# Both halves of an odd unit's transposes ahead of the sum over n, in a selective-scan block

## Chip, cores, metric

The program runs on one core of a Trainium2 chip. The metric is the device time of one execution in microseconds (us); a kernel is judged by the median of its runs.

## What is computed

For each of 16 batches (512 time steps, 256 features) the reference takes a layer norm with a shift and scale from a condition, then two Mamba blocks, one over time forward and one over time reversed, sums and norms them, and adds a gated feed-forward net of four layers. Most of the time goes into the scan of the two Mamba blocks, with E = 512 channels and N = 64 states each:

```python
def step(h, inp):
    xt, dtt, Bt, Ct = inp
    dA = jnp.exp(dtt[:, :, None] * A)
    h = dA * h + (dtt * xt)[:, :, None] * Bt[:, None, :]
    y = jnp.einsum('ben,bn->be', h, Ct)
    return (h, y)
```

So for every channel e, state n and time t: a decay exp(dt A), a drive (dt x) B, the recurrence over t, a product with C, and a sum over n.

## The kernel before

**Tiles.** A tile holds 32 channels x 4 states on the 128 partitions, and 512 time steps along the free axis. A *unit* is four such tiles (128 channels, 4 states); a *half* is two of them (1024 columns). 16 units make a pass (128 channels, all 64 states), 8 passes make a batch: 4 groups of channels for each direction, 128 units and 256 halves in all. The program has a short body ahead of the first batch, bodies for the first and the last batch, one after the last, and a hardware loop over the 14 batches between.

**One unit, over the engines.** Each engine runs its own list of instructions in the order in which they are written, and waits on counters (semaphores) of the others.

- ACT (ScalarE) writes the decays of a unit into `state[unit % 4]` (line 1078), two units ahead.
- The drive comes in one of two ways. For an even unit DVE (VectorE) multiplies rows of dt x by rows of B that TensorE has spread over the partitions into the PSUM tile `b_ps` (`spread`, line 872; the multiply is line 1256). For an odd unit ACT and POOL (GpSimd) form the product in another layout, `v_sb` (lines 1091 and 1364), and TensorE (PE) transposes it into place: eight 128x128 transposes for each half (`drive` of the tensor engine, line 882). Both ways write the PSUM tile `driven`, which has two slots: slot h for half h of any unit.
- DVE scans each half in place in `state` (line 1267); the scan of half h frees slot h of `driven`.
- POOL multiplies the scanned half by rows of C (line 1297).
- PE sums over n into the PSUM tile `y_ps` with a 0/1 matrix (`accumulate`, line 904: eight instructions for a unit) and counts `summed`, which frees the unit's slot of `state` for the decays of the unit four later.

**The order around the change.** DVE's list goes: the two scans of an even unit, the two of the odd unit behind it, then both multiplies for the next even unit. So an odd unit's first transposed half can be written once the even unit's first scan is done, its second half once the second is, and DVE needs them for its third and fourth scan of the pair. PE's list is written by `body` (line 908). At an even unit it holds: the first half of the next odd unit's transposes, the sum of the unit before, the second half, the `spread` for the next even unit, and then side work (`side`: the projections of another batch and the feed-forward net of the previous one, spread over the units by a table). At an odd unit: the sum of the even unit, and side work. Where a pass begins (`unit % NG == 0`, `ends_pass` in the code) the sum stands ahead of both halves, since DVE must read the finished `y_ps` (line 1193) before it goes on.

`accumulate` waits until POOL has read the unit (`was_read`); `drive` waits for the scan that frees its slot:

```python
pe.wait_ge(scanned, of_body(at, HALVES, last_user(q, DRIVE_RING, HALVES) + 1) + DRIVE_RING)
...
pe.wait_ge(was_read, read_done(at, unit))
```

ACT's first part of `v_sb` for a later odd unit waits for the second half of an earlier one (`v_free`), since `v_sb` has two slots.

Of the kernel before, what the change touches and what calls it, by code (L numbers as in the profile page):

```python
# [213 lines left out]
def adaln_kernel(nc, x, win, wxp, wdt, wout, f1, h1, h2, w3, cols, rows, c_t, wmod, consts, spread_rows, out):  # L214
    ctx = ExitStack()
    with ctx:
# [163 lines left out]
        def of_body(at, per_body, index):  # L380

            return at.b * per_body + index

        def last_user(k, ring, count):

            if k >= ring:
                return k - ring
            return max(r for r in range(count) if r % ring == k) - count
# [25 lines left out]
        def v_count(at, unit):  # L414

            return of_body(at, len(PE_UNITS), len([u for u in PE_UNITS if u <= unit]))
# [268 lines left out]
        def _(pe):  # L685
# [165 lines left out]
            def side(at, unit):  # L851
                for steps, signal, emit in ((PE_Q, pe_q, network), (PE_P, pe_p, project)):
                    for s, part, name, n in steps:
                        if s != unit or not at.has(part):
                            continue
                        first = min(x[0] for x in steps if x[1:3] == (part, name))
                        mm = emit(at, part, name, s - first)
                        if n:
                            mm.then_inc(signal.sem, 1)

            def spread(at, unit):
                d, g = unit % UNITS // (UNITS // 2), unit % NG
                if unit == 0:
                    pe.wait_ge(dve_side.sem, dve_side.before(at))
                elif unit == UNITS:
                    pe.wait_ge(dve_side.sem, dve_side.done(at, "next", "BC"))
                elif unit == UNITS // 2:
                    pe.wait_ge(dve_side.sem, dve_side.done(at, "p1", "BC"))
                pe.wait_ge(dve_driven, dve_drives(at, unit, 0) - 1)
                quarter = N // NN // NN  # L870
                k = slice(EG * (g // quarter), EG * (g // quarter + 1))
                pe.matmul(b_ps[:], onehot[k, g % quarter, :], b_parts[d][k, :], start=True, stop=True).then_inc(b_spread, 1)  # L872

            def drive(at, unit, h):
                q = 2 * unit + h
                if h == 0:
                    pe.wait_ge(v_made, v_count(at, unit))
                    pe.wait_ge(v_pooled, v_count(at, unit))
                pe.wait_ge(scanned, of_body(at, HALVES, last_user(q, DRIVE_RING, HALVES) + 1) + DRIVE_RING)
                for j in (2 * h, 2 * h + 1):  # L880
                    for tt in range(TT):
                        mm = pe.transpose(driven[:, q % DRIVE_RING, j % 2, tt * P:(tt + 1) * P],  # L882
                                          v_sb[:, unit // 2 % V_RING, tt, j].rearrange("p e n -> p (e n)"), ident)
                mm.then_inc(pe_driven, 1)

            def accumulate(at, unit):
                k = unit % UNITS
                nth, g = k // NG, k % NG
                if g == 0:
                    if nth:  # L890
                        pe.wait_ge(dve_side.sem, dve_side.done(at, "o0", f"Y{(nth - 1) // EC}{(nth - 1) % EC}"))
                    elif at.kind != "first":
                        pe.wait_ge(dve_side.sem, dve_side.done(at, "early", "Y13"))
                    d, c = nth // EC, nth % EC
                    if c == 0:
                        pe.wait_ge(skip_in.sem, skip_in.done(at, "o0", "skip1") if d else skip_in.before(at))
                        if d:
                            pe.wait_ge(pool_side.sem, pool_side.done(at, "p1", "ub"))
                        else:
                            pe.wait_ge(pool_side.sem, pool_side.before(at))  # L900
                    pe.matmul(y_ps[:], skip_w[:, c, :], xc_sb[d][:, c, :], start=True, stop=False)
                pe.wait_ge(was_read, read_done(at, unit))
                for j in range(JC):
                    mm = pe.matmul(y_ps[EG * j:EG * (j + 1), :], over_nn, state[:, k % STATE_RING, j, :],  # L904
                                   start=False, stop=(g == NG - 1))
                mm.then_inc(summed, 1)

            def body(at):
                scans = at.kind in SCAN_PARTS
                if at.kind == "first":  # L910
                    spread(at, 0)
                for unit in range(UNITS):
                    before_scans = unit == 0 and at.kind in ("mid", "last", "tail")
                    to_drive, ends_pass = scans and unit + 1 in PE_UNITS, unit % NG == 0
                    if to_drive and not ends_pass:
                        drive(at, unit + 1, 0)
                    if before_scans or scans and unit:
                        accumulate(at, unit - 1)
                    if to_drive and ends_pass:
                        drive(at, unit + 1, 0)  # L920
                    if to_drive:
                        drive(at, unit + 1, 1)
                        if unit + 2 < UNITS:
                            spread(at, unit + 2)
                        elif at.has("next"):
                            spread(at, unit + 2)
                    side(at, unit)

            bodies(pe, body)


# [499 lines left out]
```

## Time and profile before

| | |
|---|---|
| median of three runs | 12842.57 us |
| lowest, highest | 12838.57, 12843.2 us |
| span of the profiled execution (first to last instruction) | 12820.6 us |
| the profiled execution's own time | not given apart from its span |
| time outside the span, against the median | 22 us |
| DVE busy | 11937.2 us, 93% |
| POOL busy | 11387.8 us, 89% |
| ACT busy | 10827.8 us, 84% |
| PE busy, matmuls | 10193.9 us, 80% |
| mean granted clock of PE | 0.898 |

A page tells the busy time of each engine, and for groups of instructions how long the engine stood idle ahead of them and what ended that. Idle time matters where the engine that waits is the one that sets the pace. The timeline lists instructions by their start, each with the idle time before it. The granted clock is 1 where PE runs at its upper level and 0.5 where it runs at its lower.

### The profile page before, as it was taken

To read this page: it belongs to the slowest core of one execution; us is meant where nothing else is said; L and a number is where in the kernel's file an instruction comes from. 1 tells how busy PE (TensorE), PEld (TensorE's weight loads), DVE (VectorE), ACT (ScalarE), POOL (GpSimd) and SP (SyncE) were. 2 spreads that over 40 slices of the span, in tenths; PEclk is the share of its full clock that TensorE was granted. 3 is DMA by queue.
4 is the path that set the end of the run, shared out by engine and by line. 5 is a ranking of instruction groups with operands and counts; after the bars stand their busy time and mean duration, and the time that the engine had idled before them with its cause. 6 is when DMAs were issued, how large, how long until landed. Compare 5 with 4: busy or idle time off the path is not lost.

```text
span 12820.6 us, 179717 instructions
## 1 busy us (share of the span) xinstructions
PE 10193.9 (80%) x51484; PEld 5804.4 (45%) x51484; DVE 11937.2 (93%) x7080; ACT 10827.8 (84%) x23460; POOL 11387.8 (89%) x5924
## 2 busy tenths in 40 slices
PE   5667878888787887878878788887878878788777
PEld 2334544445444454544445444454444545444445
DVE  5999999999999999999999999999999999999992
ACT  5788888888888898888888888888888988888882
POOL 4889999999999999999998999999999999999992
PEclk7788989899898998989989898998989989899898
DMA  2223333333333343433333333333433334333332
GB/s 87 81 85 110 124 109 125 125 105 113 115 127 114 114 126 98 130 115 119 123 108 118 112 126 122 107 118 108 128 114 118 122 105 130 111 122 119 112 109 98
DMA packets 610266, 1459.04 MB, mean 114 GB/s; under 512 B 68928, under 2 KB 110032, under 8 KB 604672
## 3 DMA queue, kind: packets, MB, share of 16 engines
q1 hardware_dynamic: 609152, 1446.18, 35.3%
q8 instruction: 456, 7.47, 0.2%
q14 instruction: 658, 5.39, 0.1%
HBM read 1355.09 MB, written 90.83 MB: 113 GB/s over the span
## 4 chain that ended last, share of the span: by engine, by line
PE 28%; issue 25%; ACT 18%; DVE 18%; POOL 9%; DMA 1%; DVEq 0%; SPq 0%; POOLq 0%; ACTq 0%
DVE state L1267 11%; PE driven L882 10%; POOL state L1297 7%; ACT state L1078 6%; ACT v_sb L1091 6%; PE y_ps L904 5%; PE q_ps L837 4%; DVE driven L1256 4%; PE q_ps L824 2%; PE p_ps L745 2%; PE b_ps L872 1%; PE p_ps L753 1%; PE p_ps L769 1%; ACT L1078 1%; PE p_ps L760 1%
## 5 line engine op out<-in xcount | busy, mean ns | idle before, releaser
L1297 POOL TENSOR_TENSOR state<-state,c_rep 128x1024 f32<-128x1024 f32 x4096 | 9717.2, 2401 | 979.1 <-DVE state L1267 975.9
L1267 DVE TENSOR_TENSOR_SCAN state<-state,driven 128x1024 f32<-128x1024 f32 x4096 | 9104.4, 2270 | 405.2 <-PE driven L882 352.2
L1078 ACT ACTIVATE state<-ud_rep,cols_sb 128x512 f32<-128x512 f32 x8192 | 5211.6, 710 | 2.6 <-DMA ud_rep<-ud_rows 0.4
L1091 ACT ACTIVATE v_sb<-u_t,b_t 128x128 f32<-128x128 f32 x12288 | 4064.7, 505 | 1303.2 <-PE driven L882 1299.8
L882 PE MATMUL driven<-consts_sb,v_sb 128*128 128x128 f32 x16384 | 2641.8, 314 | 1670.0 <-DVE state L1267 1624.8
L882 PEld LDWEIGHTS driven<-consts_sb,v_sb 128*128 128x128 f32 x16384 | 2130.3, 161 | 3299.2 <-DVE state L1267 2199.8
L904 PE MATMUL y_ps<-state,consts_sb 128*32 128x512 f32 x16384 | 2452.4, 674 | 313.1 <-POOL state L1297 310.9
L1256 DVE TENSOR_TENSOR driven<-ud_rep,b_ps 128x1024 f32<-128x1024 f32 x2048 | 2390.4, 1213 | 18.2 <-DMA ud_rep<-ud_rows 18.2
L837 PE MATMUL q_ps<-hid,wq_sb 128*128 128x256 f32 x7936 | 2044.5, 403 | 140.6 <-ACT hid L1056 77.3
L837 PEld LDWEIGHTS q_ps<-hid,wq_sb 128*128 128x128 f32 x7936 | 1477.3, 196 | 838.1 <-issue 649.9
L1364 POOL TENSOR_TENSOR v_sb<-u_t,b_t 128x512 f32<-128x512 f32 x1024 | 1090.0, 1064 | 38.4 <-issue 25.4
L904 PEld LDWEIGHTS y_ps<-state,consts_sb 128*32 128x32 f32 x16384 | 338.4, 113 | 1142.1 <-POOL state L1297 643.2
L824 PE MATMUL q_ps<-xn_q,wq_sb 128*128 128x256 f32 x1984 | 518.7, 407 | 32.7 <-ACT hid L1046 19.0
L753 PE MATMUL p_ps<-u_pad,dt_sb 128*128 128x512 f32 x1024 | 508.8, 621 | 26.2 <-ACT u_pad L980 25.7
L745 PE MATMUL p_ps<-x_t,wp_sb 128*128 128x512 f32 x1024 | 500.1, 612 | 30.2 <-ACT xc L984 17.4
L872 PE MATMUL b_ps<-b_parts,onehot 32*128 32x512 f32 x1024 | 519.3, 507 | 0.0
L824 PEld LDWEIGHTS q_ps<-xn_q,wq_sb 128*128 128x128 f32 x1984 | 373.5, 198 | 221.7 <-issue 99.1
L847 PE MATMUL q_ps<-wq_sb,hid 128*128 128x256 f32 x992 | 274.6, 425 | 69.7 <-ACT hid L1061 66.1
L753 PEld LDWEIGHTS p_ps<-u_pad,dt_sb 128*128 128x128 f32 x1024 | 186.4, 195 | 239.6 <-issue 184.1
L745 PEld LDWEIGHTS p_ps<-x_t,wp_sb 128*128 128x128 f32 x1024 | 187.7, 192 | 230.5 <-issue 150.7
L790 PE MATMUL p_ps<-sz 16*128 16x512 f32 x256 | 175.1, 769 | 145.8 <-ACT u_pad L1010 145.3
L872 PEld LDWEIGHTS b_ps<-b_parts,onehot 32*128 32x128 f32 x1024 | 191.6, 187 | 186.7 <-issue 186.7
(141 smaller groups left out, 5538.1 us busy)
## 6 DMA issues: line engine op xcount, KB each, us to landing
c_rep<-bc_rows SPq DMA_DIRECT2D x2048, 256.0 KB, 3.0
ud_rep<-ud_rows SPq DMA_DIRECT2D x512, 512.0 KB, 4.1
wq_sb<-in_h SPq DMA_DIRECT2D x512, 512.0 KB, 3.7
wq_sb<-in_f SPq DMA_DIRECT2D x128, 512.0 KB, 4.2
wp_sb<-in_win SPq DMA_DIRECT2D x64, 512.0 KB, 4.5
dt_sb<-conv_taps SPq DMA_DIRECT2D x32, 1024.0 KB, 5.2
ud_rows<-u_pad SPq DMA_DIRECT2D x128, 256.0 KB, 3.4
ud_rows<-dt_sb SPq DMA_DIRECT2D x128, 256.0 KB, 3.5
```

What stands on the lines that cost most here:

```text
L745: mm = pe.matmul(p_ps[:], wp_sb[:, m, k, :], x_t[:, k, :], start=(k == 0), stop=(k == DC - 1))
L824: mm = pe.matmul(bank[:, which * TH:(which + 1) * TH], w[:, m % 2, which, k, :], n_t[:, k, i * TH:(i + 1) * TH], start=(k == 0), stop=(k = ...
L837: mm = pe.matmul(bank[:, 0:TH], w[:, k, :], src[:, k, :], start=(k == 0), stop=(k == HC - 1))
L872: pe.matmul(b_ps[:], onehot[k, g % quarter, :], b_parts[d][k, :], start=True, stop=True).then_inc(b_spread, 1)
L882: mm = pe.transpose(driven[:, q % DRIVE_RING, j % 2, tt * P:(tt + 1) * P], v_sb[:, unit // 2 % V_RING, tt, j].rearrange("p e n -> p (e n)" ...
L904: mm = pe.matmul(y_ps[EG * j:EG * (j + 1), :], over_nn, state[:, k % STATE_RING, j, :], start=False, stop=(g == NG - 1))
L1078: ins = act.activation(state[:, unit % STATE_RING, j, :], ud_rep[:, nth % 2, j, 1, :], ACT.Exp, scale=a_neg[:, d, c, j, g:g + 1])
L1091: ins = act.activation(v_sb[:, unit // 2 % V_RING, tt, :, :, n].rearrange("p j e -> p (j e)"), u_t[:, nth % 2, tt, :], ACT.Identity, scale ...
L1256: dve.tensor_tensor(driven[:, h], u_rows(unit)[:, 2 * h:2 * h + 2], b_ps[:].unsqueeze(1).to_broadcast([P, 2, T]), ALU.mult).then_inc(dve_d ...
L1267: dve.tensor_tensor_scan(flat, flat, driven[:, q % DRIVE_RING].rearrange("p j t -> p (j t)"), 0.0, ALU.mult, ALU.add).then_inc(scanned, 1)
L1297: pool.tensor_tensor(part, part, c_rep[:, unit % ROW_RING, :].unsqueeze(1).to_broadcast([P, 2, T]), ALU.mult).then_inc(was_read, 1)
L1364: pool.tensor_tensor(v_sb[:, unit // 2 % V_RING, TT - 1].rearrange("p j e n -> p (j e) n"), u_t[:, nth % 2, TT - 1, :].unsqueeze(2).to_bro ...
```

## The change

In the tensor engine's list, at an even unit that does not begin a pass, the second half of the transposes moves from behind the sum to directly behind the first half. At units that begin a pass the order stays as it was. Nothing else changes: the same instructions with the same waits.

```diff
--- before.py
+++ after.py
@@ -914,12 +914,13 @@
                     to_drive, ends_pass = scans and unit + 1 in PE_UNITS, unit % NG == 0
                     if to_drive and not ends_pass:
                         drive(at, unit + 1, 0)
+                        drive(at, unit + 1, 1)
                     if before_scans or scans and unit:
                         accumulate(at, unit - 1)
                     if to_drive and ends_pass:
                         drive(at, unit + 1, 0)
+                        drive(at, unit + 1, 1)
                     if to_drive:
-                        drive(at, unit + 1, 1)
                         if unit + 2 < UNITS:
                             spread(at, unit + 2)
                         elif at.has("next"):
```

PE in the loop over the middle batches, units 10 and 11 (`driven` is written by the transposes, `y_ps` by the sum, `b_ps` by `spread`; the last matmuls into `p_ps` are side work, and REGISTER_ALU rows work out values to wait for). Before:

```order
L879 REGISTER_ALU
L882 MATMUL driven<-consts_sb,v_sb 128x128 x8
L902 REGISTER_ALU
L904 MATMUL y_ps<-state,consts_sb 32x512 x4
L882 MATMUL driven<-consts_sb,v_sb 128x128 x8
L869 REGISTER_ALU
L872 MATMUL b_ps<-b_parts,onehot 128x512
L782 ISA
L784 MATMUL p_ps<-consts_sb,u_nat 128x128 x4
L902 REGISTER_ALU
L904 MATMUL y_ps<-state,consts_sb 32x512 x4
```

And with the change:

```order
L879 REGISTER_ALU
L882 MATMUL driven<-consts_sb,v_sb 128x128 x8
L879 REGISTER_ALU
L882 MATMUL driven<-consts_sb,v_sb 128x128 x8
L904 MATMUL y_ps<-state,consts_sb 32x512 x4
L869 REGISTER_ALU
L872 MATMUL b_ps<-b_parts,onehot 128x512
L782 ISA
L784 MATMUL p_ps<-consts_sb,u_nat 128x128 x4
L902 REGISTER_ALU
L904 MATMUL y_ps<-state,consts_sb 32x512 x4
```

The second group of eight transposes has passed the four-fold sum of unit 9; the spread, the side work and the sum of unit 10 keep their places behind it.

PE in the same loop, units 82 and 83, where side work of both kinds follows (`q_ps` belongs to the feed-forward net, `p_ps` to the projections). Before:

```order
L882 MATMUL driven<-consts_sb,v_sb 128x128 x8
L902 REGISTER_ALU
L904 MATMUL y_ps<-state,consts_sb 32x512 x4
L882 MATMUL driven<-consts_sb,v_sb 128x128 x8
L869 REGISTER_ALU
L872 MATMUL b_ps<-b_parts,onehot 128x512
L714 REGISTER_ALU
L824 MATMUL q_ps<-xn_q,wq_sb 128x256 x4
L714 REGISTER_ALU
L741 REGISTER_ALU
L745 MATMUL p_ps<-x_t,wp_sb 128x512 x2
```

And with the change:

```order
L882 MATMUL driven<-consts_sb,v_sb 128x128 x8
L879 REGISTER_ALU
L882 MATMUL driven<-consts_sb,v_sb 128x128 x8
L904 MATMUL y_ps<-state,consts_sb 32x512 x4
L869 REGISTER_ALU
L872 MATMUL b_ps<-b_parts,onehot 128x512
L714 REGISTER_ALU
L824 MATMUL q_ps<-xn_q,wq_sb 128x256 x4
L714 REGISTER_ALU
L741 REGISTER_ALU
L745 MATMUL p_ps<-x_t,wp_sb 128x512 x2
```

Again only the sum and the second half have changed places; the side work now follows the sum and the spread.

## Rows read from the trace of the kernel before

**Rows 1.** Page of the profile, its head and busy time of each engine.

```profile
span 12820.6 us, 179717 instructions
PE 10193.9 (80%) x51484; PEld 5804.4 (45%) x51484; DVE 11937.2 (93%) x7080; ACT 10827.8 (84%) x23460; POOL 11387.8 (89%) x5924
```

**Rows 2.** Waits, whole run: who <- whom, us in total, times, longest.

```profile
PE driven L882 <- DVE state L1267: 1624.8, 745, 10.1
ACT v_sb L1091 <- PE driven L882: 1299.8, 521, 7.4
...
DVE state L1267 <- PE driven L882: 352.2, 464, 3.0
```

**Rows 3.** Groups by line: busy us, mean ns | idle before <- releasers.

```profile
L1297 POOL TENSOR_TENSOR state<-state,c_rep 128x1024 f32<-128x1024 f32 x4096 | 9717.2, 2401 | 979.1 <-DVE state L1267 975.9
...
L1078 ACT ACTIVATE state<-ud_rep,cols_sb 128x512 f32<-128x512 f32 x8192 | 5211.6, 710 | 2.6 <-DMA ud_rep<-ud_rows 0.4
```

**Rows 4.** Waits of DVE in the seventh batch, 4827.7 to 5605 us.

```profile
DVE state L1267 <- PE driven L882: 22.7, 27, 3.0
```

**Rows 5.** Timeline, units 10 and 11: start, us, instruction [idle before <- releaser].

```profile
4887.28 2.39 POOL L1297 TENSOR_TENSOR state<-state,c_rep 128x1024 f32<-128x1024 f32 x1
...
4889.44 6.64 DVE L1267 TENSOR_TENSOR_SCAN state<-state,driven 128x1024 f32<-128x1024 f32 x3
...
4891.78 1.97 PE L882 MATMUL driven<-consts_sb,v_sb 128*128 128x128 f32 x8 [5.64 <-DVE state L1267]
...
4893.68 1.94 PE L904 MATMUL y_ps<-state,consts_sb 128*32 128x512 f32 x8
...
4895.55 1.97 PE L882 MATMUL driven<-consts_sb,v_sb 128*128 128x128 f32 x8
...
4897.45 0.54 PE L872 MATMUL b_ps<-b_parts,onehot 32*128 32x512 f32 x1
4897.56 2.29 DVE L1267 TENSOR_TENSOR_SCAN state<-state,driven 128x1024 f32<-128x1024 f32 x1 [1.48 <-PE driven L882]
4897.56 2.58 ACT L1091 ACTIVATE v_sb<-u_t,b_t 128x128 f32<-128x128 f32 x8 [4.71 <-PE driven L882]
...
4900.46 1.93 ACT L1078 ACTIVATE state<-ud_rep,cols_sb 128x512 f32<-128x512 f32 x3
```

**Rows 6.** Timeline, same batch: first and last wait ahead of a fourth scan.

```profile
4847.15 2.29 DVE L1267 TENSOR_TENSOR_SCAN state<-state,driven 128x1024 f32<-128x1024 f32 x1 [0.91 <-PE driven L882]
...
5564.70 2.29 DVE L1267 TENSOR_TENSOR_SCAN state<-state,driven 128x1024 f32<-128x1024 f32 x1 [0.27 <-PE driven L882]
```

**Rows 7.** Waits of DVE in units 0 to 15, 4827.7 to 4928.7 us.

```profile
DVE state L1267 <- PE driven L882: 5.8, 5, 1.5
```

**Rows 8.** Windows, units 0-15, 80-95: us, PE PEld DVE ACT POOL, PEclk.

```profile
4827.70:4928.70 101.00, 70.98 (x334) 37.00 (x326) 94.70 (x60) 72.67 (x169) 94.20 (x54) 0.75 0.38 122
...
5318.00:5424.00 106.00, 96.94 (x485) 54.15 (x484) 101.23 (x58) 98.17 (x214) 99.89 (x48) 0.98 0.40 122
```

**Rows 9.** Timeline of units 82 to 84, a packed pair.

```profile
5330.35 8.81 DVE L1267 TENSOR_TENSOR_SCAN state<-state,driven 128x1024 f32<-128x1024 f32 x4
...
5332.69 1.09 PE L882 MATMUL driven<-consts_sb,v_sb 128*128 128x128 f32 x8 [0.69 <-DVE state L1267]
...
5333.71 1.06 PE L904 MATMUL y_ps<-state,consts_sb 128*32 128x512 f32 x8
...
5341.33 8.81 DVE L1267 TENSOR_TENSOR_SCAN state<-state,driven 128x1024 f32<-128x1024 f32 x4
...
5344.50 1.03 PE L882 MATMUL driven<-consts_sb,v_sb 128*128 128x128 f32 x8
```

**Rows 10.** Timeline of PE, first and last packed first half of the batch.

```profile
5001.43 1.04 PE L882 MATMUL driven<-consts_sb,v_sb 128*128 128x128 f32 x8
...
5539.03 1.04 PE L882 MATMUL driven<-consts_sb,v_sb 128*128 128x128 f32 x8
```

**Rows 11.** Line 1267 by itself: idle before it until, us, times.

```profile
  ACT state L1078: 10.4, 24
```

## The prediction

> **What bounds the kernel now.** The first view is the page's list of engines: VectorE (DVE) is busy 11937.2 of 12820.6 us, 93%, more than any other engine [rows 1]. What is worth having is therefore what DVE waits for. The second view, the waits over the whole run, gives it: DVE's scans stood still for 352.2 us, in 464 places, until a bank of `driven` had been filled by TensorE (PE) [rows 2]. That is the most that this change can win. The third view, the groups by line, tells who is not in the way: POOL waited 975.9 us for DVE's scans, so it has room for a faster DVE, and ACT's decays waited for next to nothing (2.6 us) [rows 3].
>
> The fourth view is the timeline. The batches of the middle body are alike, so I take one, the seventh (4827.7 to 5605 us), and multiply by 16: its DVE waits for PE come to 22.7 us in 27 places [rows 4], times 16 is 363, against 352.2 for the run. I call two units, an even one and the odd one behind it, a pair: DVE runs four scans (even 0, even 1, odd 0, odd 1) and two multiplies for the next even unit. A wait ahead of the third scan is a wait for the first half of the transposes, one ahead of the fourth for the second half.
>
> The pair of units 10 and 11 shows the second kind [rows 5]. The first scan starts at 4889.44; three scans in 6.64 us with a step of 2.18 put the ends at 4891.72, 4893.90 and 4896.08. PE transposes the first half from 4891.78 in 1.97 us, does the sum of unit 9 (line 904) from 4893.68 in 1.94, and only at 4895.55 begins the second half, 1.65 us after its bank was free. It ends at 4897.5, and DVE has sat idle for 1.48 us. In the batch there are 15 such waits ahead of a fourth scan, from 0.91 at unit 3 to 0.27 at unit 121 [rows 6]; they sum to 11.2 us. In units 0 to 15 nothing else holds DVE up for PE: 5.8 us in 5 places [rows 7]. The other 12 waits, 11.5 us, stand ahead of a third scan.
>
> The clock tells the two kinds of pair apart. In units 0 to 15 the granted clock was 0.75, in units 80 to 95 0.98 [rows 8]. Eight transposes take 1.97 us at the lower level (1.2 GHz) and 1.09 at the upper (2.4 GHz), the sum 1.94 and 1.06 [rows 5, 9]. At the upper level first half and sum end 2.1 us after the first scan, within the 2.18 of the second, and the second half is not late.
>
> **What the change removes.** Outside a pass's first unit, the second half follows the first at once, and the sum stands behind both. For units 10 and 11 the second half would run from 4893.96 to 4895.93, ahead of 4896.08: the wait is gone. The other 14 have the same form, and 11.2 x 16 = **179 us** go. Where a unit begins a pass, both halves already stand together behind the sum, and nothing moves.
>
> **What it adds.** No instruction is added or dropped; the sum and the matmul of line 872 (`spread`) behind it come later. There are three prices.
>
> First, PE no longer fills its wait for the second scan with the sum. In rows 5 PE sits idle for 5.64 us up to 4891.78, although POOL's last read of unit 9 ended at 4889.67 (4887.28 + 2.39): the sum was ready 2.1 us earlier and did not pass the transposes ahead of it. So what stands behind a waiting transpose waits too. The Trainium skill says the same and speaks against this change: "TensorE: Matmul & The Clock Gate", under "Step-by-step: what each phase is for", has it that only weight loads are pulled ahead while matmuls keep program order; were the sum free to slip forward, this price would be nothing and the change would give the full 179 us.
>
> At the upper level the delay is one sum, 1.06 us, for all that PE does until the next pair. In most pairs PE then has idle time that takes it up (1624.8 us over the run waiting for scans [rows 2]). In a packed pair it has none. Units 82 and 83: before their first half PE waits 0.69 us, and after it there is no idle time until the next first half, at 5344.50 instead of the 5343.61 at which its bank was free (5341.33 + 2.28) [rows 9]. That half ends at 5345.53, 0.26 ahead of the second scan (5341.33 + 2.28 + 2.18 = 5345.79). Delayed by 1.06 it is 0.80 late, and DVE pays that. In the batch five first halves follow on so packed a stretch: those for units 29, 33, 85, 101 and 117, the first at 5001.43 and the last at 5539.03 [rows 10]. I price them at 1.06, 1.06, 0.80, 1.06 (0.80, and the remaining 0.26 one pair later) and 0.80, with 0.26 more for a delay that is carried on: 5.0 us, times 16 is **81 us**. The bounds are nothing, if the short waits of PE for ACT inside these stretches shrink by as much, and twice as much, if five more pairs that have only such waits to give pay as well. I take the middle, since rows 9 hold no idle time at all.
>
> Second, the sum delays `spread`, and DVE's multiply needs its result. At the lower level the new order has the second half end at 4895.93, the sum at 4897.8 and `spread` (0.54) at 4898.4; the fourth scan, without its wait, ends at 4898.26. That is a new wait of 0.15 us. Only pairs that stay at the lower level throughout pay it, which are those with a wait near the 1.48 of rows 5, four of the 15: 0.6 us, times 16 is **10 us**; the bounds are 0 and 15 x 0.15 x 16 = 36.
>
> Third, the sum releases the state slot that ACT's decays fill next. In rows 5 the sum of unit 9 ends at 4895.62 and the decays that need its slot begin at 4900.46, 4.8 us later. The delay is 2.2 us at the lower level, so I cost it at nothing: ACT's own order covers it. If ACT came sooner, DVE would still have its lead. ACT also gains: it waited 4.71 us for the second half there, and 1299.8 over the run [rows 2, 5]; that shortens a wait, and DVE does not wait for that work. POOL's and SP's queues are passed by nothing that moves.
>
> **Sum.** -179 + 81 + 10 = -88 us. The profiled execution's span is 12820.6; the median of the runs, 12842.57, lies 22 us above it, and I take that remainder as unchanged: 12842.6 - 88 = **12755 us**.
>
> **Rivals.** *(A) The delay is absorbed everywhere.* ACT gets its buffers earlier, PE waits less for ACT in the packed stretches, and only the gain stays: 12842.6 - 179 = 12664. For it speak ACT's 1299.8 us of waiting; against it the rows without any idle time. Chance 0.16.
>
> *(B) Ten packed pairs instead of five.* Then 161 us go back, and -179 + 161 + 10 = -8: 12835, no change. For it speaks that PE waited for DVE in only 745 places ahead of a half [rows 2], of 2048 halves in the run (16 batches of 64 pairs), so PE often has no idle time to give; against it, that many of the others had waits for POOL or ACT in between. Chance 0.14.
>
> *(C) ACT becomes the wait: slower.* Side work of an even unit now leaves PE 1.06 us later at the upper level, ACT stands in order behind it, and the decays queued behind that eviction come late for the scan. DVE has waited for decays already, 10.4 us in 24 places [rows 11], so in some units their lead is small. It decides from 6 places a batch on (88 / 1.06 / 16 = 5.2); at 8 it costs 8 x 1.06 x 16 = 136 us, and the time is 12842.6 - 88 + 136 = 12891. Against it: the decays themselves waited for nobody [rows 3], and 10.4 us is little beside 352.2. Chance 0.08.
>
> *(D) The clock falls in a packed pair.* PE now pauses about 1.0 us between the halves at the upper level. In units 80 to 95 it was busy 96.94 of 106 us [rows 8], some 10 us a pair; transposes and sums take 0.9 us more at the lower level per group of eight, and with all of its work so stretched such a pair would last some 7 us longer. One a batch costs 112 us: 12842.6 - 88 + 112 = 12867. Before the change these stretches hold the upper level, and the pause is shorter than the 5.64 us that preceded lower-level transposes [rows 5]. The skill's same page, under "A second HAM failure mode: psum-queue depth-cycling", reports frequent small idles between groups of matmuls as a cause of a swinging clock; by that rule this rival would be the likely one. Chance 0.05.
>
> **How the numbers follow.** The forecast has the rest, 0.57. What a measurement here can tell from no change is about 0.2%, 26 us. The forecast and A lie beyond that on the fast side, 0.73; B and D, at -8 and +24, are within it, 0.19; C is slower, 0.08. The range takes in A, B and the bounds of the second price, and leaves C, D and little else outside: 12655 to 12838.
>
> **What would show it.** In the profile after, DVE's waits ahead of a fourth scan are gone, and its waits for `driven` fall from 352.2 to about 254 us (352.2 - 179 + 81). They all stand ahead of a third scan, more of them in units 82 to 118. DVE gets a new wait of some 10 us ahead of line 1256's counterpart, for `b_ps`. PE waits longer in all before its second halves and less before its first. ACT's wait at `v_sb` shrinks. I am wrong if DVE's waits for ACT's decays grow by over 88 us, if the granted clock of units 80 to 95 falls below 0.9, or if waits ahead of a third scan grow past 350.

## The result and the profile after

The changed kernel took **12886.86 us** (median of five runs, 12879.91 to 12894.58) against 12838.57 of the kernel before beside it: a ratio of 1.0038, 95% interval 1.0026 to 1.0051. It is slower by 48 us, where 88 less were predicted; the time lies outside the range given.

The head of the page after, and from its fifth part the group of DVE's scans (busy us, mean ns, then idle us ahead and its releaser):

```profile
span 12885.1 us, 179717 instructions
PE 10259.9 (80%) x51484; PEld 5938.8 (46%) x51484; DVE 11996.8 (93%) x7080; ACT 10879.2 (84%) x23460; POOL 11351.8 (88%) x5924
...
L1268 DVE TENSOR_TENSOR_SCAN state<-state,driven 128x1024 f32<-128x1024 f32 x4096 | 9083.3, 2269 | 330.4 <-PE driven L882 259.9
```

Its waits over the whole run, to be laid beside [rows 2]:

```profile
PE driven L882 <- DVE state L1268: 1837.8, 1281, 10.1
...
ACT v_sb L1092 <- PE driven L882: 1015.0, 394, 7.2
...
DVE state L1268 <- PE driven L882: 259.9, 268, 3.1
```

What was forecast for the transposes happened. DVE's waits for `driven` fell from 352.2 us in 464 places [rows 2] to 259.9 in 268; 254 was forecast. In units 0 to 15 of the seventh batch, where [rows 7] had 5.8 us, none is left. ACT waits 285 us less at `v_sb`. Yet the span is 64.5 us longer (12885.1 against 12820.6). That is more than the 48 us between the medians, since the kernel before was profiled in an execution quicker than its median. DVE sets the pace, so the place to look is DVE's other instructions. Of the kernel before, by line:

```profile
L1193 DVE TENSOR_TENSOR xc<-y_ps,sz 128x512 f32<-128x512 f32 x128 | 86.4, 675 | 16.6 <-PE y_ps L904 16.5
...
L1217 DVE TENSOR_TENSOR xa<-xa,mod_p 128x1024 f32<-128x1024 f32 x16 | 45.9, 2869 | 5.7 <-ACT xa L963 5.7
...
L1223 DVE TENSOR_TENSOR o_sb<-o_sb,mod_q 128x1024 f32<-128x1024 f32 x16 | 29.6, 1852 | 5.6 <-ACT o_sb L963 5.6
...
L1238 DVE SCALAR_TENSOR_TENSOR u_pad<-sz,u_pad 128x2048 f32<-128x2048 f32 x32 | 78.2, 2445 | 65.8 <-ACT sz L1016 65.8
L1240 DVE TENSOR_TENSOR dt_sb<-dt_sb,u_pad 128x2048 f32<-128x2048 f32 x32 | 108.1, 3378 | 1.1
```

And after:

```profile
L1194 DVE TENSOR_TENSOR xc<-y_ps,sz 128x512 f32<-128x512 f32 x128 | 86.5, 676 | 55.8 <-PE y_ps L904 55.8
...
L1218 DVE TENSOR_TENSOR xa<-xa,mod_p 128x1024 f32<-128x1024 f32 x16 | 38.3, 2396 | 22.4 <-ACT xa L964 22.4
...
L1224 DVE TENSOR_TENSOR o_sb<-o_sb,mod_q 128x1024 f32<-128x1024 f32 x16 | 90.7, 5671 | 5.6 <-ACT o_sb L964 5.6
...
L1239 DVE SCALAR_TENSOR_TENSOR u_pad<-sz,u_pad 128x2048 f32<-128x2048 f32 x32 | 113.5, 3547 | 67.6 <-ACT sz L1017 67.6
L1241 DVE TENSOR_TENSOR dt_sb<-dt_sb,u_pad 128x2048 f32<-128x2048 f32 x32 | 85.7, 2678 | 1.1
L1257 DVE TENSOR_TENSOR driven<-ud_rep,b_ps 128x1024 f32<-128x1024 f32 x2048 | 2394.1, 1215 | 36.4 <-DMA ud_rep<-ud_rows 18.4 <-PE b_ps L872 15.6
```

The account of DVE's 64.5 us, from these lines:

| | us |
|---|---|
| scans' waits for `driven` | -92.3 |
| multiply waits for `b_ps` (none shown before) | +15.6 |
| line 1224 (`mix`) is itself longer, 29.6 to 90.7 busy | +61.1 |
| line 1194 waits for `y_ps` | +39.3 |
| line 1218 waits for ACT | +16.7 |
| lines 1239 and 1241 together | +12.9 |
| all else, by difference | +11.2 |

The first two were forecast, at -98 and +10. The next two, `mix` and `y_ps`, were not, and are more than the whole gain.

**`mix`.** It multiplies the block's output by a row once a batch, behind unit 15; both inputs lie in SBUF. POOL's *reads* are its products of a scanned half with rows of C (line 1297 before, 1298 after). DVE and POOL there in the seventh batch, before (start, us, instruction):

```profile
4922.95 4.69 POOL L1297 TENSOR_TENSOR state<-state,c_rep 128x1024 f32<-128x1024 f32 x2
4926.10 2.63 DVE L1223 TENSOR_TENSOR o_sb<-o_sb,mod_q 128x1024 f32<-128x1024 f32 x1
4927.61 2.02 POOL L1364 TENSOR_TENSOR v_sb<-u_t,b_t 128x512 f32<-128x512 f32 x1
```

And after:

```profile
4915.28 2.40 POOL L1336 TENSOR_TENSOR x_q<-x_q,xn_q 128x1024 f32<-128x1024 f32 x1
4917.60 4.71 POOL L1298 TENSOR_TENSOR state<-state,c_rep 128x1024 f32<-128x1024 f32 x2
4917.71 6.68 DVE L1224 TENSOR_TENSOR o_sb<-o_sb,mod_q 128x1024 f32<-128x1024 f32 x1
4922.24 1.06 POOL L1365 TENSOR_TENSOR v_sb<-u_t,b_t 128x512 f32<-128x512 f32 x1
```

Before, `mix` started late in POOL's reads and ended 1.1 us after them. After, it started 0.1 us behind the first of two reads and ended 1.1 us after the third POOL instruction (4923.30). No idle time is booked ahead of it: the time stands in the instruction's own duration.

**`y_ps`.** PE around units 30 to 32 of the same batch, before:

```profile
5014.34 1.09 PE L882 MATMUL driven<-consts_sb,v_sb 128*128 128x128 f32 x8 [1.47 <-DVE state L1267]
5015.36 1.06 PE L904 MATMUL y_ps<-state,consts_sb 128*32 128x512 f32 x8
5016.52 1.09 PE L882 MATMUL driven<-consts_sb,v_sb 128*128 128x128 f32 x8
```

After, with DVE's line 1194, which needs the pass's finished `y_ps`:

```profile
5010.62 1.09 PE L882 MATMUL driven<-consts_sb,v_sb 128*128 128x128 f32 x8 [1.47 <-DVE state L1268]
5012.80 1.52 PE L882 MATMUL driven<-consts_sb,v_sb 128*128 128x128 f32 x8 [1.08 <-DVE state L1268]
5014.25 1.94 PE L904 MATMUL y_ps<-state,consts_sb 128*32 128x512 f32 x8
...
5025.09 1.07 PE L904 MATMUL y_ps<-state,consts_sb 128*32 128x512 f32 x8
...
5026.23 0.69 DVE L1194 TENSOR_TENSOR xc<-y_ps,sz 128x512 f32<-128x512 f32 x1 [2.49 <-PE y_ps L904]
```

Before, PE worked without idle time: half 1.09, sum 1.06, half 1.09, all at the upper level. After, it pauses 1.08 us between the halves; the second half takes 1.52, between the 1.09 and 1.97 of the two levels, and the sum 1.94, which is the lower level's [rows 5]. PE has no idle time from there to the sum of unit 31, so that one is late too, by more than 1.06 us, and DVE waits 2.49 us for it at unit 32. Of the 55.8 us of these waits 34.9 are at unit 32, where there was none before.

The stretch that the prediction watched for this shows nothing of it (units 0 to 15 and 80 to 95, columns as in [rows 8]): 0.98 in units 80 to 95, as before. For the whole run the clock went from 0.898 to 0.891.

```profile
4825.00:4926.00 101.00, 68.95 (x326) 37.33 (x326) 100.02 (x61) 73.32 (x169) 93.12 (x53) 0.77 0.36 120
5320.00:5426.00 106.00, 95.59 (x484) 53.97 (x482) 100.73 (x57) 97.55 (x213) 98.09 (x48) 0.98 0.37 119
```

### The profile page after: what moved, and what is told of

Its sections match the earlier page's. It is cut to its first block, busy times and chain, and to the rows that moved or that the text cites. A ratio compares the mean times of both kernels' runs of the same rounds, so it can differ in the third digit from the quotient of the medians.

```text
span 12885.1 us, 179717 instructions
## 1 busy us (share of the span) xinstructions
PE 10259.9 (80%) x51484; PEld 5938.8 (46%) x51484; DVE 11996.8 (93%) x7080; ACT 10879.2 (84%) x23460; POOL 11351.8 (88%) x5924
## 4 chain that ended last, share of the span: by engine, by line
PE 27%; issue 27%; DVE 20%; ACT 20%; POOL 5%; DMA 1%; DVEq 1%; SPq 0%; POOLq 0%; ACTq 0%
DVE state L1268 13%; ACT state L1079 7%; PE driven L882 6%; ACT v_sb L1092 6%; PE q_ps L837 5%; PE y_ps L904 5%; POOL state L1298 4%; DVE driven L1257 4%; PE q_ps L824 2%; PE p_ps L745 2%; PE b_ps L872 2%; PE p_ps L753 1%; ACT L1079 1%; PE p_ps L760 1%; PE p_ps L769 1%
## 5 line engine op out<-in xcount | busy, mean ns | idle before, releaser
L1268 DVE TENSOR_TENSOR_SCAN state<-state,driven 128x1024 f32<-128x1024 f32 x4096 | 9083.3, 2269 | 330.4 <-PE driven L882 259.9
L882 PE MATMUL driven<-consts_sb,v_sb 128*128 128x128 f32 x16384 | 2733.8, 325 | 1860.5 <-DVE state L1268 1837.8
L882 PEld LDWEIGHTS driven<-consts_sb,v_sb 128*128 128x128 f32 x16384 | 2260.8, 168 | 2656.2 <-DVE state L1268 2180.8
L904 PE MATMUL y_ps<-state,consts_sb 128*32 128x512 f32 x16384 | 2391.0, 659 | 178.9 <-POOL state L1298 178.0
L1257 DVE TENSOR_TENSOR driven<-ud_rep,b_ps 128x1024 f32<-128x1024 f32 x2048 | 2394.1, 1215 | 36.4 <-DMA ud_rep<-ud_rows 18.4
L1057 ACT ACTIVATE hid<-q_ps,cols_sb 128x256 f32<-128x256 f32 x496 | 226.3, 456 | 203.8 <-PE q_ps L837 201.7
L1047 ACT ACTIVATE hid<-q_ps,cols_sb 128x256 f32<-128x256 f32 x496 | 204.0, 463 | 102.5 <-PE q_ps L824 99.6
```

Source lines behind the costliest of these rows:

```text
L1257: dve.tensor_tensor(driven[:, h], u_rows(unit)[:, 2 * h:2 * h + 2], b_ps[:].unsqueeze(1).to_broadcast([P, 2, T]), ALU.mult).then_inc(dve_d ...
L1268: dve.tensor_tensor_scan(flat, flat, driven[:, q % DRIVE_RING].rearrange("p j t -> p (j t)"), 0.0, ALU.mult, ALU.add).then_inc(scanned, 1)
```

## The experiments

Twelve kernels, in three groups of four, each with the kernel before beside it (12825.13, 12826.84 and 12831.79 us). Most apply the new order at a list of units only:

```diff
                     if to_drive and not ends_pass:
                         drive(at, unit + 1, 0)
+                        if unit in BOTH_AT:
+                            drive(at, unit + 1, 1)
...
                     if to_drive:
-                        drive(at, unit + 1, 1)
+                        if ends_pass or unit not in BOTH_AT:
+                            drive(at, unit + 1, 1)
```

| kernel | new order at | other edit | us | ratio, 95% |
|---|---|---|---|---|
| before_nomix | none | no `mix` | 12754.35 | 0.9924 to 0.9957 |
| after_nomix | all | no `mix` | 12810.02 | 0.9978 to 0.9997 |
| low1 | 2 to 14 | | 12801.16 | 0.9965 to 0.9988 |
| low2 | 12 units from 20 to 120 | | 12916.85 | 1.0052 to 1.0086 |
| low1_no14 | 2 to 12 | | 12799.57 | 0.9972 to 0.9991 |
| low1_pre16 | 2 to 14 | `pre2` later | 12779.72 | 0.9952 to 0.9977 |
| before_pre16 | none | `pre2` later | 12781.07 | 0.9958 to 0.998 |
| low2_fill | as low2 | pause filled | 13043.74 | 1.0154 to 1.0188 |
| only30 | 30 | | 12869.9 | 1.0019 to 1.004 |
| only30_fill | 30 | pause filled | 12847.88 | 1.0002 to 1.0021 |
| after_mixbn | all | `mix` to bn_stats | 12817.99 | 0.9976 to 0.9995 |
| pre16_4u | 2, 4, 10, 12 | `pre2` later | 12782.05 | 0.9947 to 0.9976 |

### `mix` left out, in both orders

```diff
-                    emit(dve.tensor_tensor(o_sb[:], o_sb[:], over_tiles(mod_q[:, 0, :]), ALU.mult), True)
+                    emit(dve.memset(o_sb[:, 0, 0:1], 0.0), True)
```

> Order of before; the row multiplication called mix (DVE, unit 15) is left out, a memset of one column stands in its place. Theory P (a DVE instruction with both inputs in SBUF is held out while POOL runs its reads back to back): the 16 mixes took 29.6 us of DVE, so at most 29 us go, 12811 us, or less if POOL's backlog shows at the next such instruction. Theory T (only TensorE's lateness costs): the same 29 us.

> Order of the change, mix left out in the same way. P: the 90.7 us that the 16 mixes took after the change go, 12887 - 90 = 12797 us, and the change is then no slower than the kernel before without mix (about -14 us against 12811). T: mix only sat in time that was lost anyway, so the change stays about 48 us slower than the kernel before without mix, near 12860.

Neither theory had these times: in the old order 71 us went, where 29 were the most expected, and in the new order the time lies between those of P and T. Without `mix` the new order is still 55.7 us slower than the old (12810.02 - 12754.35). So the lengthening of `mix` is a real part of DVE's account, but not the sole cause. With it gone, line 1194 waits 57.0 us for `y_ps` against 12.2 without the new order, and line 1218 27.8 us for ACT against 5.7.

The 57.0 us lie elsewhere than the 55.8 of the changed kernel: 18.4 are at unit 16, where that one waits for nothing, and 15.3 at unit 32. At unit 30 of after_nomix PE pauses as before, yet here the second half keeps the upper level:

```profile
4988.09 1.09 PE L882 MATMUL driven<-consts_sb,v_sb 128*128 128x128 f32 x8 [1.47 <-DVE state L1268]
4990.27 1.09 PE L882 MATMUL driven<-consts_sb,v_sb 128*128 128x128 f32 x8 [1.08 <-DVE state L1268]
```

So it is in 14 of the 15 batches behind the first, and the wait at unit 32 is 0.93 or 0.94 us in each of the 14. The pause alone does not decide whether the clock falls.

### Early units alone, later low-clock units alone

> New order only at units 2 to 14 of a batch, old order elsewhere. Before, 5.8 us a batch of waits ahead of a fourth scan stood there. P: they go, but DVE then reaches mix ahead of POOL's reads and waits there instead; mix grows from 1.9 us to 5 or 6, and the time stays at 12840 within 20 us. T: 5.8 x 16 = 93 us go, 12747 us.

> New order only at units 20, 22, 36, 38, 44, 52, 60, 66, 70, 74, 106 and 120, old order elsewhere. About 5.4 us a batch of waits ahead of a fourth scan stood there, 87 us in all. P: they go, less some 14 us at the instructions with two SBUF inputs of unit 40: 12767 us. T: all 87 us, 12753 us. Both expect a clear gain.

Low1 gains 24 us, between the 93 of T and the nothing of P, and outside the bounds of both. In its profile, of an execution that took 12825.57 us and so gained nothing, pairs 2, 4, 10 and 12 are shorter by 0.57, 0.73, 1.03 and 0.73 us (mean of 14 batches); pair 14 is longer by 2.83, `mix` being 5.5 us there, as P had it.

Low2 was chosen where DVE had waited for second halves, so it should have gained. Those waits shrank (idle time ahead of fourth scans 177 us to 107), but those ahead of third scans grew by more (218 to 293), and it is 0.7% slower, at a mean clock of 0.879. By line, the waits that grew most besides are line 1221's for ACT's norm (47.4 us against 5.7) and the multiply's for `b_ps` (26.9 against none). PE from unit 66 of the seventh batch in low2 (line 883 the transposes, 905 the sum, 838 side work):

```profile
5273.87 1.20 PE L883 MATMUL driven<-consts_sb,v_sb 128*128 128x128 f32 x8 [4.42 <-DVE state L1271]
5276.05 1.97 PE L883 MATMUL driven<-consts_sb,v_sb 128*128 128x128 f32 x8 [0.97 <-DVE state L1271]
5277.95 1.93 PE L905 MATMUL y_ps<-state,consts_sb 128*32 128x512 f32 x8
...
5280.53 3.78 PE L838 MATMUL q_ps<-hid,wq_sb 128*128 128x256 f32 x8
```

And before:

```profile
5234.48 1.97 PE L882 MATMUL driven<-consts_sb,v_sb 128*128 128x128 f32 x8 [4.43 <-DVE state L1267]
5236.38 1.94 PE L904 MATMUL y_ps<-state,consts_sb 128*32 128x512 f32 x8
5238.25 1.40 PE L882 MATMUL driven<-consts_sb,v_sb 128*128 128x128 f32 x8
...
5240.00 1.99 PE L837 MATMUL q_ps<-hid,wq_sb 128*128 128x256 f32 x8
```

Before, PE worked without a pause from the first half on and came back to the upper level during the second half (1.40). In low2 it paused 0.97 us, and second half, sum, spread and side work all ran at the lower level; the side group took 3.78 us and not 1.99. In pair 68, behind it, ACT's norm is then late for line 1221 by 2.98 us. That gave theory K: the pause costs clock, and the lateness is paid in the next pairs. These rows do not show it by themselves, since the first half took 1.20 us in low2, over the 1.09 of the upper level: the clock was falling ahead of the pause, behind 4.42 us without work.

### Which unit brings `mix` to its bad place, and POOL's backlog

`PRE_AT` sets the units of three pieces of POOL's early work:

```diff
-O1_AT, MIX_AT, N_AT, PRE_AT = 3, 15, 24, (5, 7, 14)
+O1_AT, MIX_AT, N_AT, PRE_AT = 3, 15, 24, (5, 7, 16)
```

> The new order at units 2, 4, 6, 8, 10 and 12 alone (the run with unit 14 as well took 12801.2 against 12825.1 of the kernel before; there pairs 2 to 12 were shorter by 0.57, 0.73, 0.06, 0, 1.03 and 0.73 us, and pair 14 longer by 2.83). Theory P (at unit 14 the DVE multiplication mix, both of whose inputs are in SBUF, now starts among POOL's reads and takes 5.7 us in place of 1.9): without unit 14 mix keeps its 1.9 us, and 12801.2 - 2.83 x 16 = 12756 us, against 12825 about 0.994 to 0.995. Rival L (time won is given back at the next fixed obstacle, mix only being the first): the time stays at about 12801, the give-back appears at unit 14 or 16 all the same.

> The new order at units 2 to 14, and POOL's third piece of early work (pre2) two units later, behind mix. Theory P with POOL's backlog as the cause (POOL is busy 94 of 101 us in units 0 to 15, so its reads run back to back when mix starts): 2.4 us less backlog lets mix start in a gap, mix falls from 5.7 towards 2 us, pair 14 gets its gain of 0.84 as well: 12801.2 - (2.83 + 0.84) x 16 = 12742 us. Rival P2 (two reads of POOL in a row catch mix whatever the backlog): mix stays over 5 us and the time near 12801.

> Control: the order of before, with pre2 two units later. Theory P: mix was 1.9 us and its floor is 1.2 to 1.4, so at most 0.6 x 16 = 10 us are won: 12815 to 12830. If POOL's backlog in units 0 to 15 held DVE in some other way as well, more is won.

> A version that might beat both: pre2 two units later (12781.1 by itself) and the new order at units 2, 4, 10 and 12 alone, where the pairs were shorter by 0.8, 1.2, 1.4 and 0.4 us. If mix stays below 3 us: 12781 - 3.8 x 16 + 1.6 x 16 = 12746. Rival R (POOL sets the pace of units 0 to 15: what DVE gains there it loses at mix): about 12780, mix near 3.8 us.

The mean of `mix` by kernel: 1.85 us before, 5.48 in low1, 4.69 in low1_no14, 3.79 in low1_pre16, 3.64 in pre16_4u, 1.37 in before_pre16. Leaving unit 14 alone did not save it: 12799.57, where P expected 12756 and rival L about 12801. So it is not one unit's order: in each of the kernels where DVE gains in units 2 to 12, `mix` is long, which fits with DVE's advance over POOL as the cause. Less backlog on POOL shortens it, but not to 2 us, as theory P had it, nor does it stay over 5, as P2 had it: 3.79 and 3.64. (L names two different rivals in these runs, as each text says.)

Rival R of the last run gave both its numbers (12780 and 3.8), but not for its reason, that DVE loses at `mix` what it gains. By the profiles, pairs 2 to 12 of pre16_4u are 3.6 us a batch shorter than those of before_pre16 and pair 14 is only 1.0 longer. What cancels the rest are 3.0 us at later pairs, whose order is the same in both, such as 38 and 68 (0.73 and 0.74); the mean granted clock is 0.898 and 0.903. That POOL sets the pace of units 0 to 15 is not shown.

Moving `pre2` helps by itself, by more than the control's expectation (12815 to 12830): 12781.07 against 12826.84. `mix` is only 8 us of it ((1852 - 1367) ns x 16); by the profiles 15 us are waits for `driven` (337.5) and 19 are line 1217 (26.9 busy against 45.9). None of the gain lies in units 0 to 17, which together keep their length within 0.1 us a batch; 4.0 us a batch lie later, 1.5 of them at pair 68, while the granted clock went from 0.898 to 0.903. Why these later places improved was not tried. On top of it the new order at early units adds nothing: 12779.72 and 12782.05. All three beat both kernels, and the smallest edit does it.

### The pause filled

Four repeats of `spread`'s matmul between the halves; the real one overwrites their result:

```diff
                         if unit in BOTH_AT:
+                            filler(at, unit + 2, 4)
                             drive(at, unit + 1, 1)
...
+            def filler(at, unit, times):
+                pe.wait_ge(dve_driven, dve_drives(at, unit, 0) - 1)
+                d, g = unit // (UNITS // 2), unit % NG
+                k = slice(EG * (g // (N // NN // NN)), EG * (g // (N // NN // NN) + 1))
+                for _ in range(times):
+                    pe.matmul(b_ps[:], onehot[k, g % (N // NN // NN), :], b_parts[d][k, :], start=True, stop=True)
```

> The new order at units 20, 22, 36, 38, 44, 52, 60, 66, 70, 74, 106 and 120, with four repeats of the matmul that spreads B (its result is written over later by the real one) between the two halves there. Without the repeats this set took 12916.9 us at a mean granted clock of 0.879, and the second halves at units 60, 66, 70, 74, 106 and 120 all ran at the lower level. Theory K (it is the pause between the halves that keeps TensorE at the lower level; second half, sum and the side group behind them then take twice as long and the next pairs are late): with the pause filled the clock is back to 0.893 or more, side groups of 8 take 2.0 us and not 3.8, pair 68 loses its 2.8 us, and the time falls to 12825 to 12860, the fourth-scan waits being back. Rival L (the lateness of the sum and of what is queued behind it is the cause): the repeats make all of that later by 1 to 2 us more, so the time is 12917 or above.

This missed in its time, 13043.74, and in its clock, 0.875. At unit 66 the fill took 2.07 us, since the clock had already begun to fall in the first half, and so it made the second half late itself: DVE's waits for `driven` rose from 359.2 to 513.1. Behind that, the side group is back to 1.99 us:

```profile
5319.08 2.07 PE L892 MATMUL b_ps<-b_parts,onehot 32*128 32x512 f32 x4
5321.08 1.97 PE L883 MATMUL driven<-consts_sb,v_sb 128*128 128x128 f32 x8
5322.98 1.94 PE L912 MATMUL y_ps<-state,consts_sb 128*32 128x512 f32 x8
...
5325.45 1.99 PE L838 MATMUL q_ps<-hid,wq_sb 128*128 128x256 f32 x8
```

The time is what rival L had (12917 or above), the side group what K had, and the fill changed both at once, so it does not decide between them. The clean place is pair 30, which stands at the upper level and has no wait to win.

> The new order at unit 30 alone, the last but one pair of a pass, where no wait ahead of a fourth scan is to be won. Theory K (the pause between the halves drops TensorE to its lower level; second half and sum then take about 0.9 and 0.7 us more, on top of the 1.06 of the moved sum, and the finished y_ps that DVE needs at unit 32 is 2.6 us late): pair 32 is longer by 2.4 us as in the changed kernel, 2.4 x 14 to 16 = 34 to 38 us, so 12860 to 12865 against 12827, about 1.0028. Rival A (pair 32 of the changed kernel is late because of what happened in units before 30): the time stays within 10 us of the kernel before.

> The same, with four repeats of the matmul that spreads B between the two halves (1.25 us at the upper level in an earlier run, so that they fit in the pause of 1.08 us within 0.2). Theory K: with the pause filled the second half takes 1.09 us and the sum 1.07, only the 1.06 us of the moved sum are left, and the wait at unit 32 shrinks from 2.5 to about 1 us: 12827 + 0.9 x 15 = 12840. Rival L (the order alone makes the sum late): as long as without the repeats, 12860 to 12865, since the repeats shorten nothing.

Both times came close to theory K. The order alone is 38 us above the kernel before beside it (33 to 38 expected) and the filled one 16 (13 expected), where rival L had no gain from the fill. PE and line 1197 or 1205 around pair 30 of the seventh batch, the order alone:

```profile
5026.10 1.09 PE L883 MATMUL driven<-consts_sb,v_sb 128*128 128x128 f32 x8 [1.46 <-DVE state L1271]
5028.28 1.50 PE L883 MATMUL driven<-consts_sb,v_sb 128*128 128x128 f32 x8 [1.09 <-DVE state L1271]
5029.71 1.94 PE L905 MATMUL y_ps<-state,consts_sb 128*32 128x512 f32 x8
...
5041.70 0.69 DVE L1197 TENSOR_TENSOR xc<-y_ps,sz 128x512 f32<-128x512 f32 x1 [2.49 <-PE y_ps L905]
```

And filled:

```profile
5023.06 1.20 PE L892 MATMUL b_ps<-b_parts,onehot 32*128 32x512 f32 x4
5024.21 1.09 PE L883 MATMUL driven<-consts_sb,v_sb 128*128 128x128 f32 x8
5025.24 1.06 PE L912 MATMUL y_ps<-state,consts_sb 128*32 128x512 f32 x8
...
5036.06 0.69 DVE L1205 TENSOR_TENSOR xc<-y_ps,sz 128x512 f32<-128x512 f32 x1 [0.93 <-PE y_ps L912]
```

More work between the halves made the wait shorter, 0.93 for 2.49. The batches behind the first split the same way within each kernel: in only30 nine of 15 had a second half of 1.5 us or more and a wait of 2.36 to 2.49, the other six had 1.09 and 0.93 to 0.94. With the fill, the lower level came in two of 15; in the changed kernel, in twelve; before, in none. So of the 2.49 us, 0.93 is the moved sum and the rest the clock.

### `mix` with one input

```diff
-                    emit(dve.tensor_tensor(o_sb[:], o_sb[:], over_tiles(mod_q[:, 0, :]), ALU.mult), True)
+                    for tt in range(TT - 1):
+                        dve.bn_stats(stats[:, 1, tt, :], o_sb[:, tt, :])
+                    emit(dve.bn_stats(stats[:, 1, TT - 1, :], o_sb[:, TT - 1, :]), True)
```

> The changed kernel with mix (o_sb times a row, both from SBUF) replaced by four bn_stats over the same 1024 columns of o_sb, which have one input; the multiplication with the row is left out. Theory P (an instruction of DVE with two inputs in SBUF stands still while POOL's reads follow one another, one with a single input does not): the four take 0.4 us each, 1.6 together, in place of 5.7, and the time is 12887 - 4 x 16 = 12820 to 12825. Rival Q (any DVE instruction at this place is slowed by POOL's traffic): they take 4 us or more together and the time stays above 12860.

The new order in full, with the same columns read at the same place by an instruction with one input. Its rows, by line:

```profile
L1225 DVE BATCH_NORM_STATS2 small<-o_sb 128x6 f32<-128x256 f32 x48 | 17.2, 413 | 5.6 <-ACT o_sb L964 5.6
L1226 DVE BATCH_NORM_STATS2 small<-o_sb 128x6 f32<-128x256 f32 x16 | 6.5, 408 | 0.0
```

Each takes 0.41 us, none over 0.43, among the same POOL reads, and the time is 12817.99 (12820 to 12825 expected), 14 us below the kernel before beside it, as after_nomix was 15 below its own. The four differ from `mix` in more than the second input: they are shorter, and they write six columns where `mix` writes 1024. The changed kernel's own rows speak to that (duration in ns, lowest/median/highest):

```profile
L1268 DVE TENSOR_TENSOR_SCAN state<-state,driven x4096: 2257/2262/2290, 167.1 to 12628.5; 128x1024 f32<-128x1024 f32 x196
...
L1224 DVE TENSOR_TENSOR o_sb<-o_sb,mod_q x16: 1227/6574/7042, 1006.2 to 12658.4; 128x1024 f32<-128x1024 f32 x16
```

The scans write 1024 columns into SBUF too and last longer than `mix` at its shortest, but read one input from SBUF and one from PSUM; more than half of them had POOL at work for over 95% of their length, and none grew past 2.29 us. So the lengthening goes with the two inputs in SBUF. The Trainium skill, "SBUF — State Buffer", section "SBUF: two separate sides", has it that of such a DVE instruction and a GpSimd instruction that reads SBUF, the one that starts first shuts the other out for its whole length. The runs agree, but for one thing: in the rows of `mix` above it was passed by two POOL instructions that started after it.

## Why the prediction was wrong

**The three terms of the sum were right in size.** Counted over the whole trace, whatever ended it, DVE's idle time ahead of fourth scans went from 177 us to nothing (179 forecast), and that ahead of third scans grew from 218 to 305, by 87 (81). The multiply's wait for `b_ps` is 15.6 (10). The 87 are luck in part: of the five units priced, 29, 85, 101 and 117 paid 48 us and 33 nothing, since DVE waits for `y_ps` at unit 32 first; the rest came at units not named, such as 57 and 79 (13 us each). None of the three signs of being wrong came: the waits for decays are 14.4 us, the clock of units 80 to 95 is 0.98, and third scans stay under 350. So the failure lies in what the sum left out.

**Failed: "No instruction is added or dropped", read as "no instruction changes its length".** Only waits were summed, and durations were carried over. `mix` alone went from 1.85 to 5.67 us, 61 us in all. A warning stood in [rows 8]: POOL was busy 94.20 of 101 us in units 0 to 15. The prediction took POOL's room from [rows 3], 979.1 us over the whole run, an average over other stages. DVE now comes to unit 14 3.2 us earlier (pairs 2, 4, 6, 10 and 12 shorter by 0.74, 0.45, 0.22, 1.03 and 0.75, mean of 14 batches), and POOL had 6.8 us of slack in all; there it meets POOL's reads.

**Failed: "At the upper level the delay is one sum, 1.06 us".** It holds where the clock stays: DVE's wait is 0.93 us at unit 32 in six batches of only30. Where the clock falls in the pause between the halves, the second half takes 1.5 to 1.97 us and the sum up to 1.94, and DVE's wait is 2.5. Rival D had the mechanism, and was given 0.05, because it was looked for in packed pairs only; its price of 7 us a pair was too high, since pair 32 grew by 2.4. The rows of pair 30 agree in kind with the passage of the Trainium skill that it quoted ("TensorE: Matmul & The Clock Gate", "A second HAM failure mode: psum-queue depth-cycling"). Units 80 to 95 kept 0.98. The fall was at pair 30, where 1.47 us without work stand ahead of the first half.

**Failed: "In most pairs PE then has idle time that takes it up".** The idle time was sought ahead of the next transposes. But DVE also waits for the sum itself where a pass ends (+39 us), and for ACT's norm behind late side work (+17). The row was there: line 1193 already waited 16.5 us for `y_ps` before the change. The sum put this term at nothing.

**Rival C** (ACT's decays late) did not come: 10.4 us [rows 11] became 14.4. Its time, 12891, was close to the result for another reason. Its chain did come at one place it had not named: in 14 of 16 batches ACT, late behind PE's side work, ends the norm 1.20 us too late for line 1218, which is the 17 us above.

**A term without effect on the sign.** The 22 us between span and median were taken as time outside the span. The changed kernel's profiled execution took 12886.86 us with a span of 12885.1, so that time is some 1.8 us, and the rest is how far executions of one kernel lie apart.

Left open: the share of each cause in time. The causes don't add. Set against the kernel before beside each, taking `mix` away won 63 us in the changed kernel (48 above became 15 below), and 71 before the change, where it was only 29.6 us long. A shift moves the places at which the clock falls: with the same pause at pair 30, it fell in 12 of 15 batches of the changed kernel, in two of after_mixbn and in one of after_nomix. That this is why the causes don't add is argued, not tested.

## What to carry to other kernels

Before an engine is made faster in a stretch, look up the busy share of the engine beside it in that same stretch; an instruction that shares something with it can grow, and no idle time will show it. Work that fills a wait may be what keeps TensorE's clock up: when it is moved, price the work behind the new pause at both levels. And follow moved work to everyone who waits for it, not only to the engine's own next job.

## What had not been expected of the hardware

- A DVE instruction with two inputs in SBUF went from 1.2 us at its shortest to 7.0 when it met a run of POOL instructions; bn_stats, with one input, kept its 0.41 us there.
- A pause of 1.08 us between two groups of transposes that each take 1.09 at the upper level was followed by the lower level in 12 of 15 batches of the changed kernel and 9 of 15 of only30, but in 1 of 15 of after_nomix; with 1.20 us of matmuls in it, in 2 of 15.
- Moving one POOL instruction of 2.4 us two units later won 46 us (0.9958 to 0.998), by the profiles none of it in units 0 to 17, where the edit is, and with a granted clock of 0.903 for 0.898.
